# Cross-attention and FFN over 128 batches: the call order of all five engines laid out anew

## What is computed

```python
x = x + xattn(layernorm(x), ctx, ctx, igate_w, igate_b, fgate_w, fgate_b, out_w)
x = x + ffn(layernorm(x), kernel, input_scale, kernel_scale, bias)

# xattn, per batch, 8 heads of 64
ig, fg = gates(concat(q, k, v))                    # one number per position and head
cs = cumsum(log_sigmoid(fg))
log_D = where(tril, cs[:, None] - cs[None, :], -inf) + ig[None, :]
top = max(log_D, axis=-1)
C = (q @ k.T / sqrt(64)) * exp(log_D - top)
h = (C / (maximum(abs(C.sum(-1)), exp(-top)) + 1e-6)) @ v
h = (h - mean(h)) / sqrt(var(h) + 1e-5) * out_w    # per head
# ffn: a 512x512 product of values rounded to float8_e4m3fn
```

## Time and profile before

| | |
|---|---|
| median of 3 runs | 1728.18 us (1726.94 to 1734.21) |
| the profiled execution's own time | 1743.25 us |
| its span, first to last instruction | 1741.5 us |
| PE busy | 1598.6 us, 92% |
| DVE busy | 1548.9 us, 89% |
| ACT busy | 1282.7 us, 74% |
| POOL busy | 1104.4 us, 63% |

### The profile page before, as it was taken

The page is one execution under the profiler, slowest core; times in us unless marked ns, Lnnn a source line. Parts: engine busy times, 40 slices in busy tenths (PEclk is TensorE's granted clock), DMA queues, the critical chain, the costliest instruction groups (busy, mean ns, idle before and its releaser), DMA issues.

```text
span 1741.5 us, 88634 instructions
## 1 busy us (share of the span) xinstructions
PE 1598.6 (92%) x36224; PEld 1191.2 (68%) x36224; DVE 1548.9 (89%) x4157; ACT 1282.7 (74%) x3137; POOL 1104.4 (63%) x1036
## 2 busy tenths in 40 slices
PE   2779999999999999999999999999999999999985
PEld 1567777776777776777776767777777777777662
DVE  6679999999998999999999999999999899998884
ACT  3667877777787777777877778777777787777652
POOL 0056766666666666666666667766666666666774
PEclk9899999999999999999999999999999999999996
DMA  5557778777777677677776777778778777776542
GB/s 164 198 168 220 249 222 237 222 230 231 224 237 233 218 234 226 214 240 221 238 235 216 227 233 227 244 217 246 218 225 240 216 223 241 230 232 195 179 130 73
DMA packets 164022, 377.66 MB, mean 217 GB/s; under 512 B 15008, under 2 KB 16032, under 8 KB 163616
## 3 DMA queue, kind: packets, MB, share of 16 engines
q1 hardware_dynamic: 163616, 371.96, 69.2%
HBM read 304.79 MB, written 67.11 MB: 214 GB/s over the span
## 4 chain that ended last, share of the span: by engine, by line
PE 58%; DVE 21%; issue 9%; DMA 9%; ACT 2%; POOL 1%; DVEq 0%; SPq 0%; POOLq 0%; ACTq 0%
PE work L508 9%; PE y L547 9%; PE qk L476 8%; PE turn L391 6%; PE turn L402 5%; DMA o_sb<-in_x 5%; DVE dec L909 4%; DMA out<-o_sb 3%; DVE bn L963 3%; DVE o_sb L1003 3%; PE arg L445 3%; PE work L488 3%; PE y L531 2%; PE y L545 2%; DVE am L1048 2%
## 5 line engine op out<-in xcount | busy, mean ns | idle before, releaser
L1143 POOL TENSOR_TENSOR x<-x,h_r 128x512 f32<-128x512 f32 x256 | 269.3, 1052 | 261.4 <-DVE x L955 146.0
L1156 POOL TENSOR_TENSOR x<-x,w_out 128x512 f32<-128x512 f32 x256 | 360.2, 1407 | 20.1
L1161 POOL TENSOR_TENSOR x<-x,o_sb 128x512 f32<-128x512 f32 x256 | 321.2, 1276 | 38.5 <-DMA o_sb<-in_x 38.2
L508 PEld LDWEIGHTS work<-c_first,dec 128*64 128x64 f32 x4096 | 264.7, 138 | 69.2 <-issue 69.0
L508 PE MATMUL work<-c_first,dec 128*64 128x65 f32 x4096 | 290.9, 224 | 12.2 <-issue 4.8
L508 PE MATMUL work<-c_sb,dec 128*64 128x65 f32 x4096 | 292.3, 224 | 2.4 <-issue 2.3
L508 PEld LDWEIGHTS work<-c_sb,dec 128*64 128x64 f32 x4096 | 264.7, 138 | 5.3 <-issue 5.3
L476 PE MATMUL qk<-qT,kT 64*64 64x128 f32 (+1 forms) x8192 | 236.0, 250 | 34.6 <-DVE dec L909 28.6
L547 PE MATMUL y<-w_ffn,zq 128*128 128x512 bf16 x1024 | 267.2, 384 | 0.0
L1003 DVE SCALAR_TENSOR_TENSOR o_sb<-y,s_out,x 128x512 f32<-128x512 f32 x256 | 190.4, 744 | 78.1 <-PE y L547 77.2
L613 ACT ACTIVATE dec<-arg 128x384 f32<-128x384 f32 x512 | 243.2, 475 | 19.4 <-PE arg L457 18.7
(11 more groups left out here) (120 smaller groups left out, 4547.8 us busy)
## 6 DMA issues: line engine op xcount, KB each, us to landing
c_sb<-in_ctx SPq DMA_DIRECT2D x128, 520.0 KB, 6.2
x_sb<-in_x SPq DMA_DIRECT2D x128, 512.0 KB, 5.1
kT<-in_keys SPq DMA_DIRECT2D x128, 512.0 KB, 6.6
o_sb<-in_x SPq DMA_DIRECT2D x128, 512.0 KB, 4.6
out<-o_sb SPq DMA_DIRECT2D x128, 512.0 KB, 3.1
c_first<-in_ctx SPq DMA_DIRECT2D x256, 130.0 KB, 5.3
w_ffn<-in_L_ffn_kernel SPq DMA_DIRECT2D x1, 512.0 KB, 10.1
w_out<-in_L_xattn_out_w SPq DMA_DIRECT2D x1, 256.0 KB, 11.7
```

The costliest lines, as they stand in the source:

```text
L508: last = mm(work_ps[rows, u, c * W:(c + 1) * W], heads_dec[:, slot * Q:(slot + 1) * Q], src, start=True, stop=True)
L1143: pl.tensor_tensor(h, h, h_r[:, t * NH:(t + 1) * NH].unsqueeze(2).broadcast_to([P, NH, DH]), ALU.mult).then_inc(h_normed[t].sem, 1)
L1156: pl.tensor_tensor(h, h, w_out[:, :], ALU.mult).then_inc(h_scaled[t].sem, 1)
L1161: pl.tensor_tensor(x1[:, b.k % 2, t, :], x1[:, b.k % 2, t, :], o_sb[:, b.k % 2, t, :], ALU.add).then_inc(x1_set[t].sem, 1)
```

## The change

The calls of all five `slot` functions stand in another order, some with another distance d, and FIRST goes from -10 to -17. No call is added or removed; what each computes and its semaphore waits are the same. FIRST has to reach as far back as the largest distance, which is now 17 (`load_x`). The diff, cut:

```diff
-FIRST, LAST = -10, 4
+FIRST, LAST = -17, 4
...
             def slot(m):
-                if live(m + 10):
-                    load_x(m + 10)
-                if live(m - 2):
-                    load_own(m - 2)
+                if live(m + 8):
+                    load_c(m + 8)
+                if live(m + 13):
+                    load_keys(m + 13)
+                if live(m + 17):
+                    load_x(m + 17)
+                if live(m + 3):
+                    store(m + 3)
                 if live(m + 7):
-                    load_keys(m + 7)
-                if live(m + 1):
-                    load_first(m + 1)
-                if live(m + 3):
-                    load_c(m + 3)
-                if live(m - 3):
-                    store(m - 3)
+                    load_first(m + 7)
+                if live(m + 5):
+                    load_own(m + 5)
...
+                if live(m + 9):
+                    x_rstds(m + 9)
...
-                    norm_apply(m + 9, 1)
...
+                if live(m - 1):
+                    quantise(m - 1)
+                if live(m + 9):
+                    norm_apply(m + 9, 1)
...
                 if live(m - 1):
                     carried(m - 1)
+                if live(m):
+                    matrix(m, 0)
                 if scans(m + 1):
                     scan_rest(m + 1, 0)
+                if scans(m + 2):
+                    scan_a(m + 2)
                 if live(m - 2):
                     head_centre(m - 2, 1)
-                if live(m):
-                    matrix(m, 0)
+                if scans(m + 2):
+                    scan_max(m + 2)
                 if live(m - 1):
                     keep_heads(m - 1)
                     head_stats(m - 1, 0)
                     normaliser(m - 1)
+                    head_stats(m - 1, 1)
+                    normaliser_clip(m - 1)
                 if scans(m + 1):
                     scan_rest(m + 1, 1)
...
-                if live(m + 7):
-                    residual(m + 7, 1)
-                if live(m + 10):
-                    weigh_keys(m + 10)
                 if live(m + 8):
                     head_norm(m + 8, 0)
+                    head_norm(m + 8, 1)
                     scale_heads(m + 8, 0)
-                    head_norm(m + 8, 1)
                     scale_heads(m + 8, 1)
+                    residual(m + 8, 0)
+                    residual(m + 8, 1)
                 if live(m + 9):
                     head_var(m + 9)
-                if live(m + 8):
-                    residual(m + 8, 0)
+                if live(m + 11):
+                    weigh_keys(m + 11)
```

More of the change, by code:

```diff
@@ L551, in slot @@
             def slot(m, wide_z):
+                if live(m + 2):
+                    states(m + 2)
+                if scans(m + 3):
+                    scan_turn(m + 3)
+                if live(m - 1):
+                    ffn(m - 1, 1, wide_z)
+                if live(m + 9):
+                    turn_round(m + 9, 1)
                 if live(m + 3):
                     arg(m + 3, 0)
-                if scans(m + 3):
-                    scan_turn(m + 3)
-                if live(m + 9):
-                    turn_round(m + 9, 1)
-                if live(m - 1):
-                    ffn(m - 1, 1, wide_z)
                 if live(m + 2):
@@ L574, in slot @@
                     ffn_turn(m)
-                if live(m + 3):
-                    arg(m + 3, 3)
-                    scores(m + 3, 1)
                 if scans(m + 6):
                     scan_rows(m + 6)
+                if live(m + 3):
+                    scores(m + 3, 1)
+                    arg(m + 3, 3)
+                if live(m):
+                    ffn(m, 0, wide_z)
                 if live(m + 10):
                     turn_round(m + 10, 0)
-                if live(m):
-                    ffn(m, 0, wide_z)
-                if live(m + 3):
-                    states(m + 3)
             slots_by_range(pe, slot)
@@ L792, in slot @@
                     decay(m + 2, 1)
+                if live(m):
+                    head_rstd(m)
                 if live(m - 1):
@@ L795, in slot @@
                     z_apply(m - 1, 1)
-                if live(m + 10):
-                    x_rstds(m + 10)
+                if live(m + 8):
+                    keep_gates(m + 8)
                 if live(m + 2):
                     decay(m + 2, 2)
-                if live(m + 8):
-                    keep_gates(m + 8)
+                if live(m - 1):
+                    quantise(m - 1)
+                if live(m + 9):
+                    norm_apply(m + 9, 1)
+                if scans(m + 3):
+                    scan_exps(m + 3)
             slots(slot)
@@ L1056, in slot @@
                     ffn_weights(m.k - (FIRST + 4))
+                if live(m + 7):
+                    norm_scale(m + 7)
+                if live(m + 9):
+                    norm_stats(m + 9, 0)
                 if live(m - 1):
                     matrix(m - 1, 1)
+                if live(m - 4):
+                    finish(m - 4, 1)
                 if live(m + 9):
@@ L1062, in slot @@
                     mix_stats(m - 3, 0)
-                if live(m - 4):
-                    finish(m - 4, 1)
+                    mix_stats(m - 3, 1)
+                if live(m + 9):
+                    norm_moments(m + 9)
                 if live(m - 3):
-                    mix_stats(m - 3, 1)
-                if scans(m + 1):
-                    scan_max(m + 1)
+                    mix_moments(m - 3)
                 if scans(m + 2):
                     scan_sums(m + 2)
-                if live(m - 3):
-                    mix_moments(m - 3)
                 if live(m - 2):
@@ L1076, in slot @@
                     scan_exponents(m + 1)
-                if live(m + 9):
-                    norm_moments(m + 9)
                 if live(m - 3):
@@ L1092, in slot @@
                     normaliser(m - 1)
+                    head_stats(m - 1, 1)
+                    normaliser_clip(m - 1)
                 if scans(m + 1):
                     scan_rest(m + 1, 1)
-                if live(m + 8):
-                    norm_scale(m + 8)
-                if live(m - 1):
-                    normaliser_clip(m - 1)
-                if live(m + 10):
-                    norm_stats(m + 10, 0)
-                if live(m - 1):
-                    head_stats(m - 1, 1)
-                if scans(m + 2):
-                    scan_a(m + 2)
                 if live(m - 3) and wide_z:
```

37 lines of the change are left out of this document (15 added, 22 removed).

## The result

The changed kernel takes **1754.97 us** in the median of 4 runs (1751.35 to 1760.74); the kernel before took 1731.2 in the 4 runs beside it. The ratio is 1.0129, 95% interval 1.0098 to 1.0161: slower by 1.3%, where no difference was forecast. The profiled executions stand closer together than the runs, 1755.13 against 1743.25 us; that is taken up with the last experiment.

A forecast was written before the change was run, and what follows sets the result against it. TensorE was taken as the bound, VectorE close behind. Profiled 1743.25 us + 32 (start) - 34 (steady part) = 1741, as a median 1727 us, no measurable change (chance 0.38); range 1703 to 1757.

The forecast's parts named there:

- The bound, and what could be won: Steady groups: TensorE bounds at 48.8 of 51.2 us per group, so 75 us at most can be won; forecast group 50.1.
- the scattered 0.9 us: Per group in the steady part: small late arrivals and unexplained TensorE stops; 0.3 us of it was expected back.
- The start, 32 us: Fill: bias and weights ahead of the first norm_stats, plus slower filling batches, cost 32 us, bounds 28 and 36.
- Own rows, 0.4 us per group: SyncE: load_own behind store and load_first, no longer behind load_x, ends GpSimd's wait for the own rows; gain 0.4 us per group.
- The first collision gone, 1.1 us per group: VectorE: first scan_rest behind matrix no longer waits out GpSimd's L1156 and delays scores; gain 1.1 us per group.
- Packed slot, 0.5: VectorE: three scan calls in one slot ahead of keep_heads make the clip late for states; cost 0.5 us per group.
- the second rival: VectorE's second scan_rest meets GpSimd's next L1156, up to 1.1 us per group: 1761, half the groups 1744; chance 0.22.
- half way between 1701 and the forecast 1727: Rival that the steady part wins more: group 49.3 us, 1701, given as 1718 half way; chance 0.31.

The follow-up runs named there:

- the last experiment: The kernel before, unchanged, profiled a second time: 1727.53 us for this profiled execution, group 50.76; its first profiled execution took 1743.25 us.
- the kernel with both edits: Changed kernel with set-up calls in the former slots and the second scan_rest directly behind the first: 1696.83 us, ratio 0.9803 to the kernel before.
- the one with the second edit alone: Changed kernel with only the second scan_rest moved directly behind the first: 1723.41 us, ratio 0.9954 to the kernel before.

## Why the prediction was wrong

*The bound, and what could be won: right.* Without the second collision and the early set-up the group takes 49.56 us, between the 48.8 of pure work and the forecast 50.1. But the 51.2 us that the sum starts from belong to one long profile; by the second profile of the same kernel the group is 50.76, and the medians lie near that one, so some of the scattered 0.9 us was not there to be won.

*The start, 32 us: right.* 29.9 measured, 22 to 26 of it the set-up calls by three comparisons (the two runs that move it alone, and the kernel with both edits against the one with the second edit alone). The fill batch was 6.78 us where 6.9 was worked out. Batches 0, 3 and 5 came at 58.3, 78.7 and 93.9, forecast 58.0, 78.7 and 94.3.

*Own rows, 0.4 us per group (12 us): right or low.* The loads' order brings 12 us in the new kernel and 20 in the old one; part of it may lie in TensorE's `issue` stops, which I had left unpriced.

*The first collision gone, 1.1 us per group (34 us): the stop went, the price was too high.* Taking it out of the kernel before, together with the one it would have made next, brought 14 us and not 34; more `issue` waits stood in its place. Taken out alone it made the kernel slower by 0.4%. The term was mis-sized because a wait of 1.1 us was taken for a gain of 1.1 us, without asking which stop comes next.

*Packed slot, 0.5 (15 us): wrong, it costs nothing measurable.* These two errors lie in opposite directions and nearly cancel. That the kernel with both edits lands 34 us below the kernel before, the figure of the sum for the steady part, is therefore in good part luck.

*The step that failed* is the one in the second rival: "So L1048 meets the last 0.2 us of it, nearly free." I had L1048 3.0 us behind the start of `head_centre` and the end of the first `scale_heads` at 3.2. It came 3.08 behind, and GpSimd's two calls followed each other 1.00 us apart and not 1.12 as in the earlier trace rows, so the second `scale_heads` began at 3.08 too. L1048 then waited for the whole of it: 1.14 us in 29 of 31 groups and half of that in one more, in front of `finish`, 30 us in all by the run that takes it away. At 3.00 us, where the prediction had it, it is indeed free, as the run with the call ahead of the clip shows. The mechanism, the price (1.1) and the total (1761 against 1755) stood in the rival; what was wrong was the belief that 0.2 us of margin, made up of five rounded durations, is a margin, and the chance of 0.22 put on it. In the rivals' arithmetic one number is off: half way between 1701 and the forecast 1727 is 1714, not 1718. Nothing rests on it.

Sum by the runs, in per cent of the kernel before: collisions of the old order out -0.79, new loads -1.17, rest of the new order 0, set-up early +1.51, second `scan_rest` against `scale_heads` +1.75; together +1.3. These are the steps of one path of kernels from the one before to the changed one, so they give the measured +1.3 by construction. Each is uncertain by 0.2 to 0.5, and another path divides the gain otherwise: with the rest of the order first and the loads last it is -0.47 and -0.71.

What stays open: what stops TensorE in the waits called `issue`, and why they grow when a named wait is taken away. The runs show only that fewer of them come with the new loads (34.2 against 27.6 us under the old order of calls). It is open too whether the rest of the new order shortens the group, as its one profile has it.

## What to carry to other kernels

When an order puts a VectorE call between GpSimd's, place it where GpSimd waits for something that stands behind the call in VectorE's own order, as directly behind the first `scan_rest` here; a place that is free by 0.2 us on paper is not free. Price a removed stop by what is next in line, and keep one-off work from standing ahead of the whole fill: here that cost 22 to 26 us, more than the 14 that the old order's collisions were worth. When a reorder of everything loses, take it apart by engine: here the loads and the place of `matrix` and the two `scan_rest` are enough for all of the gain that the medians show.

## What the runs showed of the hardware

- Whether VectorE or GpSimd waits is decided within 0.08 us: issued 3.00 us after L955, L1048 takes 0.68 us and GpSimd's pair 2.98; issued 3.08 us after it, they take 1.82 and 2.51. Back-to-back GpSimd operations do not keep VectorE out for good: issued 0.08 us ahead of the second of them, it gets in between.
- The last 0.13 us or so of an operation in the profile do not hold up the other engine: L1048 ends 0.54 to 0.55 us after the end of the one it waited for, though alone it takes 0.68, and GpSimd's operation that waited for L1048 took 0.48 us longer where the two overlapped by 0.60 us. Whether the first lets go early or the second needs its inputs late, the rows do not tell.
- A `tensor_scalar` with one SBUF input waits just as long as a subtraction with two: 0.42 us alone, 1.55 beside GpSimd.
- In some profiles TensorE's L547 shows 114 to 117 `issue` waits of up to 0.2 us between 145 and 1590 us, 18 to 19 us in all, in others next to none, with much the same group (50.54 with them and 50.63 without; 49.56 with them and 49.68 without). Waits of 18 us would be 0.6 us per group, so they do not add to the time.
